# A fused decoder layer with a routed MoE: where the router's scores, row places and last residual norms are worked out

## The reference, cut to what matters

```
x = layernorm(x + attention(x))            # 16 heads of 64, 16 batches of 128 tokens, D = 256
x = layernorm(x + mlstm(x, ctx))           # 4 heads, gates, decay matrix
xn = layernorm(x) * gamma + beta
probs = softmax(xn @ Wr + br)              # 8 experts
scores, idx = top_k(probs, 2)
full = relu(xn @ W1[e] + b1[e]) @ W2[e] + b2[e]    # for the two experts of each token
c = relu(b1) @ W2 + b2;  c_total = c.sum(over experts)
out = sum_k scores_k * (full[idx_k] - c[idx_k] + c_total)
x = layernorm(x + out)
```

## Time and profile before

| | us |
|---|---|
| median of 3 runs (764.94 to 766.87) | 765.85 |
| the profiled execution | 768.75 |
| its span, first to last instruction | 767.0 |
| TensorE busy | 700.7 |
| VectorE busy | 472.1 |
| ScalarE busy | 332.5 |
| POOL busy | 265.8 |

### The profile page before, as it was taken

One profiled execution on the slowest core, in us unless ns is written; L12 is line 12 of the kernel. 1 busy time (PEld: TensorE's weight loads), 2 busy tenths in 40 slices (PEclk: granted clock), 3 DMA queues, 4 the chain that ended last, 5 costly groups with the idle time before them and its releaser, 6 DMA issues.

```text
span 767.0 us, 15113 instructions
## 1 busy us (share of the span) xinstructions
PE 700.7 (91%) x5090; PEld 610.8 (80%) x5091; DVE 472.1 (62%) x1094; ACT 332.5 (43%) x994; POOL 265.8 (35%) x216
## 2 busy tenths in 40 slices
PE   7799999999999999998998979999999999997980
PEld 7788897888989798896887858888888888786760
DVE  2635446577868778687858745555555555553476
ACT  5575767576676767676430212221222222121112
POOL 1200000120505033050546375176069300438664
PEclk9899999999999999999799899999999999998965
DMA  9367495641011020103141245255134411213125
GB/s 311 100 222 257 146 302 175 202 147 43 30 37 47 16 63 9 43 28 124 57 165 32 73 137 166 68 156 167 34 123 129 145 41 35 68 36 97 56 69 157
DMA packets 68496, 82.66 MB, mean 108 GB/s; under 512 B 5932, under 2 KB 59736, under 8 KB 68440
## 3 DMA queue, kind: packets, MB, share of 16 engines
q1 hardware_dynamic: 59800, 52.54, 21.4%
q0 software_dynamic: 8640, 29.38, 12.1%
HBM read 45.04 MB, written 36.86 MB: 107 GB/s over the span
## 4 chain that ended last, share of the span: by engine, by line
PE 73%; DVE 7%; ACT 7%; POOL 5%; issue 4%; DMA 2%; another core or an unknown queue 1%; POOLq 0%; SPq 0%; DVEq 0%; ACTq 0%
PE bank L1012 14%; PE bank L760 8%; PE bank L761 7%; PE bank L762 7%; PE bank L982 5%; PE bank L984 5%; PE bank L983 5%; PE bank L880 4%; PE bank L992 4%; PE bank L919 3%; PE bank L931 3%; ACT arena L1112 3%; POOL arena L729 2%; PE bank L968 1%
## 5 line engine op out<-in xcount | busy, mean ns | idle before, releaser
L1012 PE MATMUL bank<-w_ring,hidT_hi 128*128 x320 | 121.6, 413 | 6.2 <-DVE hidT_lo L1665 6.2
L1233 ACT ACTIVATE hidT_hi<-bank 128x512 fp32r<-128x512 f32 x80 | 43.5, 596 | 180.6 <-PE bank L992 171.0
L1112 ACT ACTIVATE arena<-bank,negmx 128x128 f32<-128x128 f32 x256 | 90.8, 377 | 6.2 <-DVE negmx L1268 6.2
L1012 PE MATMUL bank<-w_ring,hidT_lo 128*128 x320 | 84.2, 283 | 0.0
L1638 DVE TENSOR_TENSOR arena<-bank,b_rep 128x512 f32<-128x512 f32 x80 | 55.4, 692 | 42.9 <-PE bank L984 41.3
L1644 DVE TENSOR_REDUCE work<-bank 128x256 f32<-128x512 f32 x40 | 27.7, 692 | 85.1 <-PE bank L1012 77.5
L1012 PEld LDWEIGHTS bank<-w_ring,hidT_hi 128*128 128x128 f32 x320 | 61.1, 191 | 18.2 <-issue 6.9
L982 PE MATMUL bank<-w_ring,xgT_hi 128*128 x160 | 67.3, 421 | 4.6 <-DVE xgT_lo L1657 2.8
L632 POOL TENSOR_TENSOR rsq<-ssq,neghalf 128x8 f32<-128x8 f32 x8 | 13.2, 1646 | 145.4 <-DVE ssq L1368 145.4
L984 PE MATMUL bank<-w_ring,xgT_lo 128*128 x160 | 63.5, 397 | 0.0
L983 PE MATMUL bank<-w_ring,xgT_hi 128*128 x160 | 63.2, 395 | 0.0
(11 more groups left out here) (253 smaller groups left out, 1897.3 us busy)
## 6 DMA issues: line engine op xcount, KB each, us to landing
xg_dram<-zeros SPq DMA_DIRECT2D x9, 2176.0 KB, 8.8
w_raw<-in_L_ffn_W_dram POOLq DMA_DIRECT2D x16, 1024.0 KB, 6.1
y_dram<-zeros SPq DMA_DIRECT2D x2, 2560.0 KB, 10.7
work<-xg_dram SPq DMA_DIRECT2D x40, 128.0 KB, 2.1
y_dram<-work SPq DMA_DIRECT2D x40, 128.0 KB, 1.7
b_rep<-in_L_ffn_b_dram POOLq DMA_DIRECT2D x8, 512.0 KB, 4.2
work<-gmax_dram SPq DMA_DIRECT2D x14, 256.0 KB, 3.4
arena<-in_x_dram SPq DMA_DIRECT2D x8, 256.0 KB, 2.7
```

What stands on the lines that cost most here:

```text
L1012: last = pe.matmul(o, l, r, start=c == 0 and l is both[0], stop=c == FC - 1 and l is both[0])
L1112: last = nc.scalar.activation(probs[:, n % 2, h * S:(h + 1) * S], ps_score[:, h * S:(h + 1) * S], ACT.Exp, bias=negmx[:, n % 2, h:h + 1], ...
```

## The change

It has four parts. (1) The two chained additions to `chosen_sum` go; `chosen` becomes a tensor [128, 8 pairs, 3, 8] whose first plane holds the sum of what was chosen in the pairs before, made in one reduction per pair behind the signal to TensorE; ("R", p) gets a third matmul, and for Z the totals take three instead of one. The experts' first rows come in through partition 0 of the first plane, so `find_slots` reads ranks and places in one product out of PSUM. (2) In `pick` two chained operations on 16 elements become two unchained ones on 8, with a scalar per partition. (3) Reciprocal, scores and `wgt` leave the pair's chain: scores for all pairs are made at once in `rows_of_y`, `wgt` in three operations behind tiles 28, 29 and 30. (4) `both_norms` no longer normalises `xres` of the pairs A, Y and Z; that happens behind the same three tiles, doubled at once, and POOL doubles the other ten batches only.

```diff
-    pool.tensor_tensor(rstd2[:, :], var2[:, :], neghalf[:, 0:4], ALU.pow).then_inc(rstd2_ready, 1)
+    pool.tensor_tensor(rstd2_of[max(0, p - A)][:, :], var2[:, :], neghalf[:, 0:4], ALU.pow).then_inc(rstd2_ready, 1)
...
-        pool.tensor_tensor(xres[:, :, :], xres[:, :, :], xres[:, :, :], ALU.add).then_inc(input_doubled, 1)
+        most = xres[:, 0:2 * A, :]
+        pool.tensor_tensor(most, most, most, ALU.add).then_inc(input_doubled, 1)
...
+    if b >= 2 * A:
+        pool.wait_ge(last_normed, b // 2 - A + 1)
...
     else:
         pe.wait_ge(tri_ready, 3)
         pe.wait_ge(counts_in, p + 1)
-        pe.matmul(dst[:, 0:2 * E], tri[:, :], chosen.rearrange("p b e -> p (b e)"), start=True, stop=False)
-        last = pe.matmul(dst[:, 0:2 * E], ones[:, :],
-                         chosen_sum[:, 2 * p:2 * p + 2, :].rearrange("p b e -> p (b e)"),
+        ahead, both = chosen[:, p, 0, :], chosen[:, p, 1:3, :]
+        pe.matmul(dst[:, 0:2 * E], tri[:, :], both.rearrange("p b e -> p (b e)"), start=True, stop=False)
+        pe.matmul(dst[:, E:2 * E], ones[:, :], chosen[:, p, 1, :], start=False, stop=False)
+        last = pe.matmul(dst[:, 0:2 * E], ones[:, :], ahead.unsqueeze(1).broadcast_to([P, 2, E]),
                          start=False, stop=True)
         if p == PAIRS - 1:
-            last = pe.matmul(dst[:, 2 * E:3 * E], ones[:, :], chosen_sum[:, B, :], start=True, stop=True)
+            for k in range(3):
+                last = pe.matmul(dst[:, 2 * E:3 * E], ones[:, :], chosen[:, p, k, :], start=k == 0, stop=k == 2)
     last.then_inc(proj_done, 1)

 def scores(n):
...
+pe.wait_ge(wgt_ready, 1)
...
+    if p >= A:
+        return
     for b in range(2):
         last = dve.tensor_scalar(xres[:, 2 * p + b, :], xres[:, 2 * p + b, :], mv2[:, b, 0:1],
                                  rstd2[:, b:b + 1], ALU.subtract, ALU.mult)
     chain.link(last)
+
+def norm_of_last(k):
+
+    for b in range(2 * (A + k), 2 * (A + k) + 2):
+        last = dve.tensor_scalar(xres[:, b, :], xres[:, b, :], mv2_of[k][:, b % 2, 0:1],
+                                 twice_rstd[:, k, b % 2:b % 2 + 1], ALU.subtract, ALU.mult)
+    last.then_inc(last_normed, 1)

 def over_e(v):
     return v.unsqueeze(2).broadcast_to([P, 2, E])
...

     dve.wait_ge(route_exp_out, p + 1)
-    dve.tensor_reduce(tot, ex, AX.X, ALU.add).then_inc(tot_ready, 1)
+    dve.tensor_reduce(tot[:, 2 * p:2 * p + 2], ex, AX.X, ALU.add).then_inc(tot_ready, 1)
     pick(p, 0)
     dve.wait_ge(tot_ready, p + 1)
     chain.link(dve.scalar_tensor_tensor(ex, hot[:, 0, :, :], -2.0, ex, ALU.mult, ALU.add))

 def pick(p, k):
     pair = slice(2 * p, 2 * p + 2)
-    chain.link(dve.tensor_reduce(best[:, k, :], ex, AX.X, ALU.max))
-    chain.link(dve.tensor_tensor(is_top, ex, over_e(best[:, k, :]), ALU.is_equal))
-    chain.link(dve.tensor_tensor(is_top, is_top, over_b(em8[:, :]), ALU.mult))
+    chain.link(dve.tensor_reduce(best[:, k, pair], ex, AX.X, ALU.max))
+    for b in range(2):
+        last = dve.scalar_tensor_tensor(is_top[:, b, :], ex[:, b, :], best[:, k, 2 * p + b:2 * p + b + 1],
+                                        em8[:, :], ALU.is_equal, ALU.mult)
+    chain.link(last)
     chain.link(dve.tensor_reduce(idx[:, k, pair], is_top, AX.X, ALU.min))
     chain.link(dve.tensor_tensor(hot[:, k, :, :], over_b(em8[:, :]), over_e(idx[:, k, pair]), ALU.is_equal))

 def second_choice(p):

-    pair = slice(2 * p, 2 * p + 2)
     pick(p, 1)
-    chain.link(dve.tensor_tensor(chosen, hot[:, 0, :, :], hot[:, 1, :, :], ALU.add))
-    chain.link(dve.tensor_tensor(chosen_sum[:, 2 * p + 1, :], chosen_sum[:, 2 * p, :], chosen[:, 0, :],
-                                 ALU.add))
-    dve.tensor_tensor(chosen_sum[:, 2 * p + 2, :], chosen_sum[:, 2 * p + 1, :], chosen[:, 1, :], ALU.add)\
-        .then_inc(counts_in, 1)
-    chain.link(dve.reciprocal(inv, tot))
-    chain.link(dve.tensor_tensor(score[:, :, pair], best, inv.unsqueeze(1).broadcast_to([P, 2, 2]), ALU.mult))
-    chain.link(dve.tensor_tensor(of_hot, hot, score[:, :, pair].unsqueeze(3).broadcast_to([P, 2, 2, E]),
-                                 ALU.mult))
-    chain.link(dve.tensor_tensor(wgt[:, pair, :], of_hot[:, 0, :, :], of_hot[:, 1, :, :], ALU.add))
+    dve.tensor_tensor(chosen[:, p, 1:3, :], hot[:, 0, :, :], hot[:, 1, :, :], ALU.add).then_inc(counts_in, 1)
+    dve.wait_ge(counts_in, p + 1)
+    if p + 1 < PAIRS:
+        chain.link(dve.tensor_reduce(chosen[:, p + 1, 0, :], chosen[:, p, :, :].rearrange("p k e -> p e k"),
+                                     AX.X, ALU.add))

 def choose(p):
     first_choice(p)
...
     un = ("R", p)
     done(dve, un)
     if p == PAIRS - 1:
-        chain.link(dve.tensor_scalar(n1, ring(un)[0][:, 2 * E:3 * E], 1.0, None, ALU.add))
-    dve.tensor_tensor(rank, ring(un)[0][:, 0:2 * E].rearrange("p (b e) -> p b e", e=E),
-                      over_b(first_row[:, :]), ALU.add).then_inc(ring_free[place[un][0][0]], 1)
+        chain.link(dve.tensor_tensor(n1, ring(un)[0][:, 2 * E:3 * E], region_at[:, 0:E],
+                                     ALU.subtract))
+    rank = ring(un)[0][:, 0:2 * E].rearrange("p (b e) -> p b e", e=E)
+    dve.tensor_tensor(of_hot, hot, rank.unsqueeze(1).broadcast_to([P, 2, 2, E]), ALU.mult)\
+        .then_inc(ring_free[place[un][0][0]], 1)
     read(dve, un)
-    chain.link(dve.tensor_tensor(of_hot, hot, rank.unsqueeze(1).broadcast_to([P, 2, 2, E]), ALU.mult))
     pair = slice(2 * p, 2 * p + 2)
     chain.link(dve.tensor_reduce(row_f[:, :, pair], of_hot, AX.X, ALU.add))
     dve.tensor_copy(slot[:, :, pair], row_f[:, :, pair]).then_inc(slot_ready, 1)
...
-    chain.link(dve.tensor_tensor(shift[:, :], y_first[:, :], first_row[:, :], ALU.subtract))
-    chain.link(dve.tensor_scalar(shift[:, :], shift[:, :], 1.0, None, ALU.add))
+    chain.link(dve.tensor_tensor(shift[:, :], y_first[:, :], region_at[:, 0:E], ALU.subtract))
+    chain.link(dve.reciprocal(inv[:, :], tot[:, :]))
+    chain.link(dve.tensor_tensor(score[:, :, :], best[:, :, :], inv[:, :].unsqueeze(1).broadcast_to([P, 2, B]),
+                                 ALU.mult))
+    for k in range(3):
+        last = dve.tensor_scalar(twice_rstd[:, k, :], rstd2_of[k][:, 0:2], 2.0, None, ALU.mult)
+    chain.link(last)
...
+def weights_in(n):
+
+    which = idx[:, :, :].rearrange("p k b -> p (k b)")
+    scores_of = score[:, :, :].rearrange("p k b -> p (k b)")
+    wide_of = [P, 2 * B, E]
+    if n == 0:
+        chain.link(dve.tensor_tensor(of_idx, em8[:, :].unsqueeze(1).broadcast_to(wide_of),
+                                     which.unsqueeze(2).broadcast_to(wide_of), ALU.is_equal))
+    elif n == 1:
+        chain.link(dve.tensor_tensor(of_idx, of_idx, scores_of.unsqueeze(2).broadcast_to(wide_of), ALU.mult))
+    else:
+        dve.tensor_tensor(wgt[:, :, :], of_idx[:, 0:B, :], of_idx[:, B:2 * B, :], ALU.add).then_inc(wgt_ready, 1)
+
...
+    if j < LOOPED + 3:
+        norm_of_last(j - LOOPED)
+        weights_in(j - LOOPED)
...
+dve.wait_ge(last_normed, 3)
```

More of the change, by code:

```diff
@@ L167, in decoder_layer @@
         off[0] = 0
-        logit, ex, is_top, chosen, rank = (carve(work, 2 * E).rearrange("p (b e) -> p b e", e=E) for _ in range(5))
+        logit, ex, is_top = (carve(work, 2 * E).rearrange("p (b e) -> p b e", e=E) for _ in range(3))
         hot, of_hot = (carve(work, 4 * E).rearrange("p (k b e) -> p k b e", k=2, e=E) for _ in range(2))
-        top, tot, inv = (carve(work, 2) for _ in range(3))
-        best = carve(work, 4).rearrange("p (k b) -> p k b", k=2)
+        top = carve(work, 2)
         wide = carve(work, E * N_TILES)
@@ L208, in decoder_layer @@
         stats2 = sb("stats2", [P, 2, 6])
-        mv2 = sb("mv2", [P, 2, 2])
+        mv2_of = [sb(f"mv2_{k}", [P, 2, 2]) for k in range(3)]
         var2 = sb("var2", [P, 4])
-        rstd2 = sb("rstd2", [P, 4])
+        rstd2_of = [sb(f"rstd2_{k}", [P, 4]) for k in range(3)]
+        twice_rstd = sb("twice_rstd", [P, 3, 2])
         rboth = sb("rboth", [P, 2])
@@ L215, in decoder_layer @@
         ve4, rstd4, shift4 = ([sb(f"{name}_{k}", [P, 4]) for k in range(2)] for name in ("ve4", "rstd4", "shift4"))
+        best = sb("best", [P, 2, B])
+        tot = sb("tot", [P, B])
         score = sb("score", [P, 2, B])
@@ L221, in decoder_layer @@
         em8 = sb("em8", [P, E])
-        first_row = sb("first_row", [P, E])
+        region_at = sb("region_at", [P, E + 4])
         iotile = sb("iotile", [P, N_TILES])
         iorow = sb("iorow", [P, N_TILES])
-        chosen_sum = sb("chosen_sum", [P, B + 1, E])
+        chosen = sb("chosen", [P, PAIRS, 3, E])
         tile_row = sb("tile_row", [P, N_TILES], I32)
@@ L235, in decoder_layer @@
         shift = sb("shift", [P, E])
+        inv = sb("inv", [P, B])
         own = sb("own", [E, E])
@@ L325, in decoder_layer @@
         tot_ready = sem("tot_ready")
+        wgt_ready = sem("wgt_ready")
+        last_normed = sem("last_normed")
         route_exp_in = sem("route_exp_in")
@@ L562, in _ @@
```

(16 more changed lines are left out.)

## The result

The changed kernel takes 777.09 us (median, 774.12 to 779.15) where the kernel before, run beside it, takes 766.36 (764.94 to 769.84): ratio 1.0125, 95% interval 1.009 to 1.016. (Ratios here are the estimates on record and not quotients of two medians, which would give 1.0140.) That is 10.7 us slower by the medians and outside the range of 761.8 to 770.0. The profiled execution took 776.07 us, its span is 774.3.

A forecast was written before the change was run, and what follows sets the result against it. TensorE was taken to bound the loop and expert stage, waits between engines the drain. Terms 0.88 - 0.22 + 0 + 0 + 0.38 + 0.50 = +1.54 us gave 770.3 profiled, median 767.4; range 761.8 to 770.0.

The forecast's parts named there:

- Loop, +0.88: R of pairs 0 to 3: one matmul more each, 0.22 us on TensorE's path; bounds 0 and 1.68.
- Pair 4, -0.22: Last loop iteration: VectorE reaches L1274 sooner, so TensorE's next gate, the read of R, comes 0.22 us earlier; bounds 0, -0.9.
- pick, a gain of 0.04 each: In pick, two unchained operations and one link replace two chained ones: 0.04 us gained; bounds 0.15 gain, 0.1 loss.
- Norms of A, Y, Z, 0: Drain: VectorE's waits behind the residual norms get no shorter, so moving them saves 0 us; up to 3.15 if uncovered.
- moved work counts in full: Rival, 12%: norms and three chains are on the path, so the change saves 3.95 us in all: 761.9 us.
- Drain, +0.38: R of Y, fills, R of Z: TensorE's half-clock fills bind, not the counts, so +0.38 us; bounds -0.52 and +1.0.
- the prediction's own sign of being wrong: Drain: the forecast is wrong if R of Z follows its counts at once; they were to be ready 1.9 us earlier.
- rows_of_y: hidden: Drain: rows_of_y takes 0.55 us more, hidden by VectorE's 1.44 us idle behind it: 0 us; +0.55 without cover.
- Behind tiles 28 to 30, +0.50: Expert stage: new norms and wide operations cost 0.25 us each behind tiles 28 and 29, 0 behind 30; bounds 0, 3.7.
- Slower: the tiles' new work has no cover: Rival, 18%: behind tiles 28 to 30 VectorE holds back bias and low parts, TensorE waits in L1012: 769.0 to 770.6.
- The other sign of being wrong: Behind tiles 28 and 29: forecast wrong if TensorE's waits in L1012, taken as about 0.25 us, reach a microsecond.
- The stall at tile 35: Rival, 9%: VectorE's unexplained 7.59 us idle at tile 35 may go (5%, 761.7) or come once more (4%, 773).

The follow-up runs named there:

- the run with the norms back: Changed kernel with wide operations behind tiles 32 to 34, unlinked, and residual norms of pairs 5 to 7 again in the drain's chain: ratio to before 1.0006 (0.9988 to 1.0024).
- the PSUM input: Kernel before plus three unused 128 x 256 additions behind tile 30, first input the y bank in PSUM, second in SBUF: ratio 0.9999 (0.9979 to 1.0019).
- additions with two SBUF inputs: Kernel before plus three unused 128 x 256 additions behind tile 30, both inputs in SBUF: ratio 1.0084 (1.0051 to 1.0118).
- the reductions: Kernel before plus three unused reductions of zeros, 128 x 256 to one column each, behind tile 30: ratio 0.9991 (0.9974 to 1.0008).
- a scaling: Kernel before plus three unused tensor_scalar multiplications of 128 x 256, input and output in SBUF, behind tile 30: ratio 1.0009 (0.9991 to 1.0027).
- the added fills: Late, unlinked kernel with two pairs of loop count matmuls, 38 for 24 fills ahead of Y's xn transposes: 0.9993; also 7 for 5 and 18 for 14 ahead of R: 1.0014.

## Why the prediction was wrong

The step that failed is the tiles' new work, +0.50 in the sum: it cost 9.74 us. The prediction took VectorE's operations beside POOL as slower by a fixed 0.96 us at most, where they wait until POOL's operation is over. The terms in order:

*Loop, +0.88: right.* 45.62 to 45.83 us an iteration.

*Pair 4, -0.22: right.* R of pair 3 to the first matmul behind the places (L760, L779 after) is 46.33 before and 46.31 after, with the 0.22 of R's third pair in it: -0.24.

*pick, a gain of 0.04 each: half of it.* From the equality to the index it took 0.42 us before (361.45 to 361.87) and 0.40 after (361.47 to 361.87).

*Norms of A, Y, Z, 0: no effect found*, by the run with the norms back; the rival "moved work counts in full" falls with it. The idle times behind them grew as forecast, from 1.13, 0.34 and 0.97 us to 2.67, 0.92 and 1.54.

*Drain, +0.38: the reason was wrong, and the size can't be told from nothing.* "TensorE's fills bind" held in the one profile I had. In four other profiles of the old count code R of Y to R of Z took 5.4 to 5.7 us and R of Z waited 0.28 to 1.57 us for its counts; with the PSUM input, TensorE in order of time:
```profile
429.19 3.37 PE L940 MATMUL bank<-ident 128*128 128x128 f32 x28
434.13 0.36 PE L862 MATMUL bank<-work,tri 128*128 128x16 f32 x2 [1.56 <-DVE chosen_sum L1452]
```
So the counts do save time here: 4.99 to 5.00 us with the new code. It came back in two places: R of Z to the first transposes is about 0.6 longer (12.0 to 12.3 for 11.3 to 11.6), about what its three more pairs of matmuls take, and R of A to R of Y took 25.9 to 26.2 us in six of seven profiles with the new counts where the old have 25.0, the changed kernel's own 24.45 being an exception. R of pair 4 to the first transposes took 80.8 to 82.7 us in five profiles of the old code (mean 81.4) and 80.0 to 82.7 in six of the new, norms moved (mean 81.7). My taking one profile's half clock as a property of the kernel is the error; the 2.7 us between profiles with the same drain code are larger than the term. The two profiles compared at first had the longest drain of the old code and the shortest of the new, which is chance: R of Z waiting for its counts was the prediction's own sign of being wrong, and it came.

*rows_of_y: hidden, as taken.* The 0.6 above leaves little room for its 0.55.

*Behind tiles 28 to 30, +0.50: this step failed.* Two sizes were wrong. Tiles 28 and 29 cost 0.52 and 0.46, not 0.25 each. The bias came 0.97 us late (0.91 forecast), but the 0.43 that the prediction took as cover, from the end of the first low part (658.87) to L1012 (659.30), isn't all idle: with TensorE waiting, L1033 still starts 0.24 to 0.25 us behind that end, so 0.19 of it covers. The 0.24 to 0.26 that TensorE shows as idle is less than what it loses, since L1012 otherwise starts 0.13 us behind transposes that are recorded as 0.38 long. All of this cost goes with the wait behind the wide operation. The large one is tile 30: I had it at 0, and its bound at 0.96, "what L1408 took longer beside POOL". That row was the mechanism itself, and I read it as a slow-down of a fixed size. Its second norm ended at 386.29, 0.15 us behind this POOL operation of 1.37 us, in the kernel before:
```profile
384.77 1.37 POOL L641 TENSOR_TENSOR arena<-arena,norms 128x512 f32<-128x512 f32 x1 [1.99 <-DVE arena L1397]
```
So the price is what is left of POOL's operation. Beside the weight split these are of 1.9 and 4.5 us, and three VectorE operations in a row met three of them: with the half clock that followed, 9.95 us in that step. POOL in the kernel before, at the same place:
```profile
663.54 1.91 POOL L612 CAST w_ring<-w_raw 128x2048 fp32r<-128x2048 f32 x1
665.54 4.58 POOL L614 TENSOR_TENSOR w_ring<-w_raw,w_ring 128x2048 fp32r<-128x2048 f32 x1
```
The runs show the exclusion and which operands bring it. That it is a port is from the Trainium skill (SBUF — State Buffer, "Who interferes with whom"): VectorE's second port pair is POOL's only one; an operation with two SBUF inputs contends with a POOL operation that reads SBUF, one in a two-port mode with any, and whichever issues first blocks the other for its whole instruction. The additions with two SBUF inputs (4.72 us for 0.42), those with a PSUM input (1.07 us for three) and the reductions (1.06 for three) agree with it; the first norm behind tile 30, which started 0.53 us ahead of POOL's cast and was held all the same, does not agree with the issue order. From the two rows above, one POOL operation for each of three VectorE operations makes a bound of 1.91 + 4.58 + 1.91 = 8.4 us of waiting, not 0.96; 7.5 came, and the half clock on top.

*"Slower: the tiles' new work has no cover", 18%*, is the rival that came nearest: the place was right and POOL's split was named, but it priced the meeting with POOL at 0.96 us, a tenth of 9.95. The other sign of being wrong, TensorE waiting a microsecond in L1012 behind these tiles, came too (7.28).

*The stall at tile 35* neither went nor doubled.

Sum with measured terms: 0.88 - 0.24 + 0.1 + 9.74 + 0.6 = 11.1, against 10.7 measured. The 0.1 is the drain's 81.7 - 81.4 = 0.3 less the 0.2 of it that lies in pair 4's term already, and it is uncertain by more than its size; the 0.6 is of one pair of profiles.

## What to carry to other kernels

Before work is moved to VectorE's idle time, look at what POOL runs at that time. A VectorE operation with two SBUF inputs, or a `tensor_scalar` in SBUF, may end only when POOL's does, so its price is up to POOL's longest operation there, and each further one can meet POOL's next. A row that is longer beside another engine is read by its end: if that coincides with the other's end, take it as a wait that grows with the other's length, and test it. A long wait of TensorE can cost more than itself, since it then worked at half clock. A gain that rests on which engine binds at half clock needs more than one profile.

## What the runs showed of the hardware

- Held by POOL's cast or subtraction: norms (`tensor_scalar` with two per-partition scalars; 2.59 and 4.66 us for 0.41), additions with two SBUF inputs (2.40 and 4.72 for 0.42), a scaling (2.39 for 0.28). Not held: additions with one PSUM input (three in 1.07), reductions (three in 1.06), biases from PSUM (0.68 beside the subtraction). Held operations end 0.15 to 0.3 us behind POOL's.
- The first norm behind tile 30 started 0.53 us before POOL's cast and was held (2.59 us), in all three profiles that have it; an addition and a scaling 0.52 us before it ran in 0.42 and 0.28. POOL was issuing the DMA of `b_rep` in that time in all of them (660.86 to 661.42 in the changed kernel), so that alone doesn't explain it. I can't say why.
- A scaling by a constant of 128 x 256 takes 0.28 us, a norm with two per-partition scalars 0.41.
- TensorE's time at half clock in the drain differs between profiles of nearly the same code: after a first stretch of 6.8 or 10.2 us between 359 and 375, further ones of 3.4 or 6.8 us fall in different places. Six of the seven profiles of the new count code without the added fills have one of 6.8 us that starts between 413 and 418, at an idle time of 3.39 to 3.41 us that the seventh, the changed kernel's first, doesn't have; the two with that idle time filled have no half clock there.
